# Adaptive-norm attention and FFN block: the lo rows of the condition bias stacked under its hi rows, engine orders adapted

## What is computed

```python
# x: 32 batches x 32 tokens x 256 features; idx: one of 8 adapters for each batch
w, b = cond_weights[idx], fside[idx]                      # 32x32 and 32 numbers per batch
c = einsum('bct,bcd->bdt', x, w) + b[:, :, None]          # condition, with the condition bias b
x = x + attention(c, W_qkv, b_qkv, W_out, b_out)          # 16 heads of 16, causal
gate, up = lora(x, Wg, Ag, Bg, idx), lora(x, Wu, Au, Bu, idx)   # 256 -> 1024
y = lora(silu(gate) * up, Wd, Ad, Bd, idx)                # 1024 -> 256
hidden = fwht(silu(y @ W1.T) * (y @ W3.T))                # Walsh-Hadamard over 1024
x = x + hidden @ W2.T
```

## Time and profile before

| | us |
|---|---|
| median of three executions | 228.81 |
| the profiled execution | 228.75 |
| its span, first to last instruction | 227.0 |
| TensorE busy | 221.5 |
| GpSimd busy | 121.2 |
| ScalarE busy | 100.8 |
| VectorE busy | 84.8 |
| granted TensorE clock | 1.0 of full speed, throughout |

### The profile page before, as it was taken

One profiled execution on the slowest core, in us unless ns is written; L12 is line 12 of the kernel. 1 busy time (PEld: TensorE's weight loads), 2 busy tenths in 40 slices (PEclk: granted clock), 3 DMA queues, 4 the chain that ended last, 5 costly groups with the idle time before them and its releaser, 6 DMA issues.

```text
span 227.0 us, 3701 instructions
## 1 busy us (share of the span) xinstructions
PE 221.5 (98%) x1482; PEld 179.7 (79%) x1482; DVE 84.8 (37%) x141; ACT 100.8 (44%) x169; POOL 121.2 (53%) x93
## 2 busy tenths in 40 slices
PE   7799999999999999999999999999999999999995
PEld 2477787878788888888888888888888888888894
DVE  4988988888454342211022000202222222220211
ACT  2389798895853414756143000313355555440000
POOL 1029676637787297999993800180266667443000
PEclk9999999999999999999999999999999999999999
DMA  6956400004024100330110000031101100000211
GB/s 180 411 212 183 141 1 4 4 3 133 5 72 108 56 0 1 92 92 26 46 46 0 0 3 0 0 92 47 46 3 51 43 0 0 4 0 0 79 62 46
DMA packets 5345, 13.02 MB, mean 57 GB/s; under 512 B 720, under 2 KB 1360, under 8 KB 5072
## 3 DMA queue, kind: packets, MB, share of 16 engines
q1 hardware_dynamic: 4896, 11.72, 16.4%
q10 hardware_dynamic: 432, 1.07, 1.4%
HBM read 11.73 MB, written 1.05 MB: 56 GB/s over the span
## 4 chain that ended last, share of the span: by engine, by line
PE 94%; DVE 3%; DMA 1%; issue 0%; DVEq 0%
PE bank L385 28%; PE bank L389 28%; PE bank L387 28%; PE bank L460 3%; PE bank L485 2%; DMA index_i<-index 1%; DVE cond_sel L883 1%; DVE k_x L877 1%; PE bank L440 1%; PE bank L404 1%; PE bank L441 1%; PE bank L442 1%; PE bank L450 1%; PE bank L469 1%; PE bank L411 0%
## 5 line engine op out<-in xcount | busy, mean ns | idle before, releaser
L1172 POOL TENSOR_TENSOR h_lo<-tmp_b,h_hi 128x512 fp32r<-128x512 f32 x32 | 40.8, 1290 | 30.5 <-ACT h_hi L724 26.3
L385 PE MATMUL bank<-act_hi,w_hi 128*128 128x512 f32 x152 | 52.8, 392 | 0.1
L389 PE MATMUL bank<-act_hi,w_lo 128*128 128x512 f32 x152 | 52.4, 389 | 0.0
L387 PE MATMUL bank<-act_lo,w_hi 128*128 128x512 f32 x152 | 52.3, 389 | 0.0
L1018 DVE TENSOR_TENSOR tmp_b<-bank,tmp_a 128x512 f32<-128x512 f32 x32 | 21.1, 688 | 73.6 <-PE bank L389 56.2
L1134 POOL TENSOR_TENSOR w_lo<-raw,w_hi 128x512 fp32r<-128x512 f32 (+3 forms) x22 | 35.3, 1616 | 10.5 <-ACT w_hi L659 10.5
L385 PEld LDWEIGHTS bank<-act_hi,w_hi 128*128 128x128 f32 x152 | 28.5, 188 | 7.1 <-issue 1.1
L389 PEld LDWEIGHTS bank<-act_hi,w_lo 128*128 128x128 f32 x152 | 28.5, 188 | 6.0
L387 PEld LDWEIGHTS bank<-act_lo,w_hi 128*128 128x128 f32 x152 | 28.5, 188 | 5.7
L724 ACT ACTIVATE h_hi<-tmp_b 128x512 fp32r<-128x512 f32 x32 | 19.8, 632 | 28.4 <-DVE tmp_b L1018 28.4
L385 PE MATMUL bank<-h_hi,w_hi 128*128 128x512 f32 (+1 forms) x88 | 27.3, 370 | 0.0
(11 more groups left out here) (85 smaller groups left out, 246.1 us busy)
## 6 DMA issues: line engine op xcount, KB each, us to landing
raw<-w_stream SPq DMA_DIRECT2D x13, 256.0 KB, 2.7
raw<-w_stream SPq DMA_DIRECT2D x8, 384.0 KB, 3.2
raw<-w_stream SPq DMA_DIRECT2D x3, 512.0 KB, 3.6
k_x<-x_slots ACTq DMA_DIRECT2D x2, 512.0 KB, 6.7
tmp_b<-w_t SPq DMA_DIRECT2D x1, 1024.0 KB, 9.0
resid<-x_feat SPq DMA_DIRECT2D x1, 1024.0 KB, 10.9
out_feat<-tmp_b SPq DMA_DIRECT2D x3, 256.0 KB, 2.1
out_feat<-tmp_b SPq DMA_DIRECT2D x2, 128.0 KB, 1.8
```

What stands on the lines that cost most here:

```text
L385: pe.matmul(ps[:, :], w[0], x_hi, start=start, stop=False)
L387: pe.matmul(ps[:, :], w[0], x_lo, start=False, stop=False)
L389: last.append(pe.matmul(ps[:, :], w[1], x_hi, start=False, stop=stop))
L1172: pool.tensor_tensor(lo, tmp_b[:, n % 4, :], f32(hi), ALU.subtract).then_inc(prod_split, 1)
```

## The change

The 8 lo rows of fside are put under the hi rows, at partitions 32 to 39 of one buffer fs_both of 40 rows (the rows between are zero), and the batch's one-hot is repeated there. For this SP issues a small load of fside into rows 32 to 39 (fs_rows), second in its queue; POOL clears fs_both, makes a column adapter_row (the adapter's number for rows 0 to 31, the number less 32 below) and both parts; DVE makes the one-hot of 64 rows by comparing with adapter_row (`batch_onehots`), now behind the first `condition_product`; `condition_bias` is one DVE operation of 40 rows for each half and `conditioned_bias` one product of 40 rows for each tile. Besides, the orders of all engines and the banks in the first third of the program are other ones. The diff, cut to its core:

```diff
+LO_ROW = 32
+BIAS_ROWS = LO_ROW + N
...
     ("k", 0, 0, 5), ("fold", 0, 0, 6), ("k", 0, 1, 7), ("q", 0, 1, 0), ("s", 0, 0, 1),
-    ("s", 0, 1, 2), ("k", 1, 0, 4), ("s", 0, 2, 3), ("s", 0, 3, 6), ("q", 1, 0, 5),
...
+    ("s", 0, 1, 2), ("fold", 0, 1, 4), ("k", 1, 0, 3), ("s", 0, 2, 6), ("s", 0, 3, 5),
...
-    plan += [(name, (5, 4, 6, 3, 1, 7, 2, 0)[n % 8]) for n, name in enumerate(later)]
+    plan += [(name, (0, 5, 1, 3, 6, 7, 4, 2)[n % 8]) for n, name in enumerate(later)]
...
-        ones = sb("ones", [N, P], F32R)
+        ones = sb("ones", [BIAS_ROWS, P], F32R)
...
-        fs_hi = sb("fs_hi", [N, T], F32R)
-        fs_lo = sb("fs_lo", [N, T])
+        fs_both = sb("fs_both", [BIAS_ROWS, T], F32R)
+        fs_rows = sb("fs_rows", [BIAS_ROWS, T])
+        adapter_row = sb("adapter_row", [P, 1])
...
-        fb_hi, fb_lo = (w[0:N, RING - TOK:RING].rearrange("p (b d) -> p b d", d=T) for w in (w_hi, w_lo))
+        fbias = w_hi[0:BIAS_ROWS, RING - TOK:RING].rearrange("p (b d) -> p b d", d=T)
...
             sp.dma_start(const[:, :], first).then_inc(const_loaded, 16)
+            sp.dma_start(fs_rows[LO_ROW:BIAS_ROWS, :], first[0:N, C_FSIDE:C_FSIDE + T]).then_inc(fs_loaded, 16)
...
             def conditioned_bias(s, c):
                 pe.wait_ge(ones_made, 1)
-                pe.wait_ge(fbias_made, 2 * (s + 1))
-                for fb in (fb_hi, fb_lo):
-                    last = pe.matmul(tile("xc", s, c)[:, :], ones[:, :], fb[:, s * BH:(s + 1) * BH, :], start=False,
-                                     stop=fb is fb_lo, skip_group_check=True)
-                full(last, "xc", s, c)
+                pe.wait_ge(fbias_made, s + 1)
+                full(pe.matmul(tile("xc", s, c)[:, :], ones[:, :], fbias[:, s * BH:(s + 1) * BH, :], start=False,
+                               stop=True, skip_group_check=True), "xc", s, c)
...
             scores(0, 0)
+            fold(1)
             key(1, 0)
             scores(0, 1)
             query(1, 0)
             key(1, 1)
             v(0, 0)
             scores(1, 0)
-            fold(1)
             v(0, 1)
             query(1, 1)
             values(0, 0)
             v(1, 0)
-            scores(1, 1)
+            fold(2)
             values(0, 1)
-            fold(2)
+            v(1, 1)
             project(0, 0, 0, 1)
-            v(1, 1)
+            fold(3)
             project(0, 1, 0)
             project(0, 1, 1)
-            fold(3)
+            scores(1, 1)
+            adapters_in(0, 0, 0, 1)
+            gate_up(0, 0)
+            adapters_in(0, 1, 0)
             values(1, 0)
-            adapters_in(0, 0, 0, 1)
-            adapters_in(0, 1, 0)
-            gate_up(0, 0)
             adapters_in(0, 1, 1)
             gate_up(1, 0)
             gate_up_adapters(0, 0)
...
+            conditioned_hi(0, 0)
             split_weights(W_Q)
             split_weights(W_K)
-            conditioned_hi(0, 0)
-            fold_raw_hi(0, 1, 2)
+            split_weights(W_V)
             conditioned_hi(0, 1)
-            fold_raw_hi(3)
+            fold_raw_hi(0, 1)
             conditioned_hi(1, 0)
-            split_weights(W_V)
+            fold_raw_hi(2)
             conditioned_hi(1, 1)
             split_weights(W_OUT)
             queries(0, 0)
             keys(0, 0, 0, 1)
...
-            exps(1, 2)
             residual_hi(0, 1)
             split_weights(W_GU + 2)
+            spread_slots(1, 1)
+            evacuate_v(1, 0)
+            exps(1, 2)
+            evacuate_v(1, 1)
+            exps(1, 3)
+            split_weights(W_GU + 3)
             even_heads(1, 0)
-            evacuate_fold(3)
+            adapters_hi(0, 0)
+            split_weights(W_GU + 4)
+            adapters_hi(0, 1)
+            spread_slots(1, 2)
             even_heads(1, 1)
-            split_weights(W_GU + 3)
-            exps(1, 3)
-            adapters_hi(0, 0)
-            adapters_hi(0, 1)
+            split_weights(W_GU + 5)
             attention_hi(1, 0)
-            spread_slots(1, 2)
-            split_weights(W_GU + 4)
             gate(0, 0)
             spread_slots(1, 3)
-            split_weights(W_GU + 5)
...
-            dve.tensor_scalar(onehot_n[:, :], idx_row, const[:, C_PCOL:C_PCOL + 1], None,
-                              ALU.is_equal).then_inc(onehot_n_made, 1)
+
+            def batch_onehots():
+                dve.wait_ge(row_made, 2)
+                dve.tensor_scalar(onehot_n[0:2 * LO_ROW, :], idx_row[0:2 * LO_ROW], adapter_row[0:2 * LO_ROW, :], None,
+                                  ALU.is_equal).then_inc(onehot_n_made, 1)
...
             def condition_bias(s):
                 b = slice(s * BH, (s + 1) * BH)
                 dve.wait_ge(onehot_n_made, 1)
-                dve.wait_ge(fs_split, 2)
-                for part, fb in ((f32(fs_hi[:, :]), fb_hi), (fs_lo[:, :], fb_lo)):
-                    dve.tensor_tensor(fb[:, b], onehot_n[0:N, b].unsqueeze(2).to_broadcast([N, BH, T]),
-                                      part.unsqueeze(1).to_broadcast([N, BH, T]), ALU.mult)\
-                       .then_inc(fbias_made, 1)
+                dve.wait_ge(fs_split, 4)
+                dve.tensor_tensor(fbias[:, b], onehot_n[0:BIAS_ROWS, b].unsqueeze(2).to_broadcast([BIAS_ROWS, BH, T]),
+                                  f32(fs_both[:, :]).unsqueeze(1).to_broadcast([BIAS_ROWS, BH, T]), ALU.mult)\
+                   .then_inc(fbias_made, 1)
...
             condition_product(0)
+            batch_onehots()
             condition_sum(0)
...
+            maxima(1, 2)
+            less_maxima(1, 2)
             maxima(1, 3)
             less_maxima(1, 3)
-            odd_heads(1, 0)
-            turn(1, 2)
+            sums(1, 2)
+            inverses(1, 2)
             sums(1, 3)
             mask_adapters(0, 0)
-            odd_heads(1, 1)
+            inverses(1, 3)
+            turn(1, 2)
             mask_adapters(0, 1)
             adapters_lo(0, 0)
-            inverses(1, 3)
+            odd_heads(1, 0)
             adapters_lo(0, 1)
-            attention_lo(1, 0)
+            odd_heads(1, 1)
             turn(1, 3)
             hidden(0, 0)
...
             pool.memset(f32(ones[:, :]), 1.0).then_inc(ones_made, 1)
 
+            pool.memset(f32(fs_both[:, :]), 0.0).then_inc(fs_split, 1)
             pool.wait_ge(const_loaded, 16)
-            pool.tensor_copy(fs_hi[:, :], fside).then_inc(fs_split, 1)
             pool.wait_ge(fs_split, 1)
-            pool.tensor_tensor(fs_lo[:, :], fside, f32(fs_hi[:, :]), ALU.subtract).then_inc(fs_split, 1)
+            pool.tensor_copy(adapter_row[0:LO_ROW, :], const[0:LO_ROW, C_PCOL:C_PCOL + 1]).then_inc(row_made, 1)
+            pool.tensor_scalar(adapter_row[LO_ROW:2 * LO_ROW, :], const[LO_ROW:2 * LO_ROW, C_PCOL:C_PCOL + 1],
+                               float(LO_ROW), None, ALU.subtract).then_inc(row_made, 1)
+            pool.wait_ge(row_made, 2)
+            pool.tensor_copy(fs_both[0:N, :], const[0:N, C_FSIDE:C_FSIDE + T]).then_inc(fs_split, 1)
+            pool.wait_ge(fs_split, 2)
+            pool.wait_ge(fs_loaded, 16)
+            pool.tensor_copy(fs_both[LO_ROW:BIAS_ROWS, :], fs_rows[LO_ROW:BIAS_ROWS, :]).then_inc(fs_split, 1)
+            pool.wait_ge(fs_split, 3)
+            pool.tensor_tensor(fs_both[LO_ROW:BIAS_ROWS, :], fs_rows[LO_ROW:BIAS_ROWS, :],
+                               f32(fs_both[LO_ROW:BIAS_ROWS, :]), ALU.subtract).then_inc(fs_split, 1)
 
             def butterflies(stage, t):
...
-            pool.wait_ge(fbias_made, 4)
-            fold_raw_lo(0)
+            pool.wait_ge(fbias_made, 2)
+            fold_raw_lo(0, 1)
             weights_lo(W_OUT)
-            fold_raw_lo(1, 2, 3)
+            fold_raw_lo(2)
             weights_lo(W_A)
             weights_lo(W_GU)
-            normalised(0, 0, 1, 2)
+            normalised(0, 0)
+            fold_raw_lo(3)
+            normalised(0, 1)
             spread_first(0, 0)
+            normalised(0, 2)
+            spread_first(0, 1)
             normalised(0, 3)
-            spread_first(0, 1, 2)
-            normalised(1, 0)
-            spread_first(0, 3)
-            normalised(1, 1)
-            spread_first(1, 0, 1)
-            normalised(1, 2)
+            spread_first(0, 2, 3)
+            normalised(1, 0, 1)
             weights_lo(W_GU + 1)
             weights_lo(W_GU + 2)
-            normalised(1, 3)
-            spread_first(1, 2, 3)
+            spread_first(1, 0, 1)
+            normalised(1, 2, 3)
+            spread_first(1, 2)
+            weights_lo(W_GU + 3)
+            spread_first(1, 3)
             hidden_lo(0, 0)
-            weights_lo(W_GU + 3)
+            weights_lo(W_GU + 4)
             hidden_lo(0, 1)
             hidden_lo(0, 2)
-            weights_lo(W_GU + 4)
```

More of the change, by code:

```diff
@@ L761, in _ @@
             keys(0, 1, 0, 1)
+            fold_raw_hi(3)
             split_weights(W_A)
@@ L764, in _ @@
             split_weights(W_GU)
-            exps(0, 0)
-            keys(1, 0, 0, 1)
```

(34 more changed lines are left out.)

45 lines of the change are left out of this document (21 added, 24 removed), and 18 rows, old and new, of the table EARLY_BANKS.

## The result

The changed kernel took 230.55 us (median of nine executions) against 228.77 of the kernel before: 1.0078 times, with an interval of 1.0053 to 1.0102. It is slower by about 1.8 us where 0.7 less was forecast.

What follows compares the result with a forecast made beforehand. TensorE was taken as the bound, streaming without gaps once its run begins. Begin -0.58, bias products -0.46, order +0.35 and ties +0.05 made -0.64, so 228.1 us; forecast 227.9 to 228.4 (0.55), range 227.4 to 229.2.

Steps and rivals of the forecast that it cites:

- The begin: TensorE's unbroken run begins at 10.97, not 11.55 (-0.58), and fewer bias products save 0.46: together -1.04 us.
- The order of scores and values: Half 1's second scores and value products on TensorE, now apart, pay more changes of shape: +0.35 us, bounds 0 to 0.45.
- the first rival: More gain: changes of order on TensorE cost nothing, a stop behind half 1's values may go; 227.5 to 227.7, chance 0.12.
- Three ties: Three places where TensorE comes close to its inputs, (a), (b) and (c): +0.05 us together, bounds 0 and 0.5.
- (b): Values of half 1, first part: GpSimd's two spread operations end some 0.3 us before TensorE comes.
- (c): Gate and up with adapters: second adapter remainder ready at T + 2.93, TensorE there at T + 2.95, a tie.
- (a): Key weights' remainder on DVE: if GpSimd's 1.28 us fold remainder starts first, ends at 15.15; TensorE wants it at 15.0.
- The failed step: The program from about 60 on: only neighbours of one shape swapped, last 150 us and tail as before; no term.
- a lock that takes the gain: GpSimd starts up to 1.28 us just ahead of DVE at (c) or the second attention remainder: 228.7 to 229.4, chance 0.2.
- The signs of being wrong: Late first DVE bias product, TensorE waits at 15, 43 or 56 behind stretched DVE operations, or 0.35 missing in half 1.
- The small load: Feed of the new rows at the begin: ready at 4.4, wanted by DVE at 7.1, hidden with 2.7 us to spare.

Runs made afterwards that it cites:

- e10: Changed kernel without the stacking and small load, GpSimd's butterflies of three stages and second fold remainder moved behind: 229.04 to 229.10 us undisturbed.
- e4: Kernel before with the stacking alone (small load included), all engines' orders and banks as before: 228.57 to 229.40 us undisturbed.
- e1: Changed kernel with DVE's order mask, remainder, mask, remainder put back for z of half 1: 228.36 to 228.91 and 230.36 to 230.72 us undisturbed.
- e12: e1 with one short DVE memset (64 columns) ahead of the second remainder of z of half 1: 230.43 to 230.90 us undisturbed.
- e8: Changed kernel, all orders kept, each GpSimd butterfly replaced by four memsets of its output: 228.55 us.
- e3: Kernel before with only DVE's order for z of half 1 changed to mask, mask, remainder, remainder: 230.93 us in one undisturbed execution, median 232.52.
- e11: Kernel before with the small load alone, second in SP's queue and read by nobody: 228.96 us undisturbed, ratio 1.0016.
- e5: e4 with ScalarE's second conditioned hi part of half 0 moved ahead of W2's first three hi parts: 228.16 us, ratio 0.9972.
- e6: e5 with GpSimd's butterflies of the first three stages behind the hidden and weight remainders of their m: 228.13 us.

## Why the prediction was wrong

- **The begin** (-1.04): right. Measured -1.13: the blocks at 10.88 (10.97 forecast), since the DVE bias operation began at 7.04 and not 7.11; the two products 0.66 as forecast.
- **The order of scores and values** (+0.35): right in its rows. Values stand at 38.61 to 39.69 and scores at 45.01 to 46.51, 1.08 and 1.50 as forecast. But from the first scores (lead 0.65) to 56.14 (0.41) the order costs 0.24 net; e10 gives 0.3 by time. What the sum put at nothing is the short stop that the first rival named: before, the value products of half 1 took 1.25 to the next product (47.02 to 48.27), after 1.08 (51.51 to 52.59). These 0.17 came back.
- **Three ties** (+0.05): (b) held, and (c) within 0.05 (56.14 to the next product is 0.28, not 0.23). (a) was mis-sized. The key weights' remainder itself came at 13.15, ahead of GpSimd's 13.70, as the row of 13.20 let one hope. But I looked at that one operation and not at the small ones behind it, and took for GpSimd one remainder of 1.28 where the new order has two in a row. Measured 0.42 of wait and 0.05 of a product entered late: 0.48.
- **The failed step**: "From about 60 on only neighbours of one shape are swapped, and the last 150 us and the tail are as before." It was true of TensorE's order alone and was said of the kernel. On DVE a remainder moved behind a mask, into a stretch in which GpSimd reads for 5.2 us. It would have needed a term of its own: the row of the second remainder (82.72 before) beside that of the butterflies (79.93, 5.73 for two) shows a margin of hundredths (82.72 against 82.74), and the price as well: one butterfly of 2.4 behind the wait, against a slack of about 0.3 between 83.41 (its end) and 83.75. It was put at nothing. Measured 2.1 at the place (2.04 of standing and 0.08 for a product entered late), which made +1.8 of what was -0.36.
- **The rival that came nearest**, a lock that takes the gain, had the mechanism and the wrong sizes: "an operation of up to 1.28", from the row at 13.20, and the places (c) and attention. The longest reading operation of GpSimd beside a DVE one sets the price, and that is the butterfly. The signs of being wrong named waits at 15, 43 and 56; the one at 83 lay behind the point where the orders were no longer followed.
- **The small load**: the rows were ready at 5.52 (4.4 forecast; the copy of 1.17 at 4.02 stood in between) and wanted at 7.04. Hidden, as forecast. "With nothing on TensorE waiting for it before 16", said of W2, holds for the new order on ScalarE only, as e4 shows: the sum credited the stacking with 1.04 and the orders with a cost, while without ScalarE's order there is nothing to credit.

The account of the changed kernel: -1.13 begin, +0.48 at 20, +0.24 order and stop, +0.05 at 56 are -0.36; with 2.04 of standing at 83.4 and 0.08 of a product entered late it comes to +1.8, the difference of the spans.

## What to carry to other kernels

For each pair of operations that is swapped, on any engine and however late in the program, look at what the neighbouring engine does at that time, and price the swap by the longest operation there with which it can collide. Where two engines lock each other out, a margin of hundredths of a us bears no edit: e1 was fast by 0.02 in its trace, and 0.1 more on DVE (e12) cost it 2.1; move the long operation to where nobody waits. And when an earlier begin is to be harvested, list what is queued ahead of the next inputs on every engine, since the wait moves to the next input that hangs on a transfer.

## What the runs showed of the hardware

- DVE operations of very few elements are held as well: 128x8 took 1.28 in place of 0.15, and a tensor_scalar of 128x32, with an input of one number per partition, 1.27 in place of 0.23, each beside a GpSimd subtraction.
- A GpSimd operation that only writes does not hold them: beside memsets of 128x1024 two subtractions of 128x512 took 1.48 together (e8), beside two butterflies of the same output 3.71.
- A 1 KB load put second in SP's queue moved the next issues by 0.42. The first weights came later by much more: ScalarE, waiting for the transfer each time, began on the query weights at 6.15 and 6.32 without it (before, e3), at 7.84 with the load alone (e11), and at 8.09 to 8.80 in e4, e5 and e6. So 1.5 to 1.7 come with the load alone, in single traces; why so much more than its issue is open, and no product waited for it. How much later W2 lands is not told by them, with ScalarE's begin on it at 12.24 to 13.29 with the load and at 12.43 and 12.49 without; by time the load alone costs the kernel before 0.19 (e11).
- Behind a stall of 1.9 us TensorE's granted clock was 0.55 for 3.8 us in one profile (e12) and 1.00 in another (the changed kernel); with the fall the execution was 1.7 longer. What decides between the two is not shown.
